# Causal attention in an eight-batch transformer block: the diagonal mask moves from TensorE to GpSimd, and the row maximum is found in two parts

## What is computed

```
def _L1_attn_ref(x, Wq, Wk, Wv, Wo, bo, rel_emb):
    NUM_HEADS, CLIP = 16, 16
    q, k, v = ...                       # x @ W, split into 16 heads of 16 features
    dist = jnp.clip(jnp.abs(r[None, :] - r[:, None]), 0, CLIP)
    scores = jnp.einsum('bhqd,bhkd->bhqk', q, k) * rel_emb[dist]
    causal = jnp.triu(jnp.ones((s, s), dtype=bool), k=1)
    scores = jnp.where(causal, -jnp.inf, scores)
    attn = jax.nn.softmax(scores / np.sqrt(hd), axis=-1)
    ctx = jnp.einsum('bhqk,bhkd->bhqd', attn, v)
    return ctx @ Wo + bo
```

## Time and profile before

| | |
|---|---|
| median of 3 runs | 3185.65 us |
| the profiled execution: its own time | 3191.0 us |
| its span, first to last instruction | 3189.3 us |
| mean granted clock of PE | 0.946 |
| the mask products of the attention phase touched | 512, from 2334.8 to 2857.6 us of the span |

### The profile page before, as it was taken

How to read it: one execution, slowest core, us unless ns; L and a number is a source line. 1 busy time by engine, 2 the same in 40 slices (tenths; PEclk the granted TensorE clock), 3 DMA queues, 4 the chain that set the end, 5 groups by cost and what they waited for, 6 DMA issues and landing times. The chain is left out here.

```text
span 3189.3 us, 54032 instructions
## 1 busy us (share of the span) xinstructions
PE 2881.4 (90%) x19465; PEld 2047.0 (64%) x19465; DVE 1665.2 (52%) x4524; ACT 1528.2 (48%) x2579; POOL 1339.6 (42%) x1331
## 2 busy tenths in 40 slices
PE   4899999767899999668999997999879999988999
PEld 4799999722344333257999996666546666655666
DVE  4411111168888888554111111566676666655666
ACT  1133333247988888611333332333247777772333
POOL 3544444358999999435444443000043444320000
PEclk9899999978999999868999998999989999999999
DMA  8199999800544444861999997100052333301000
GB/s 281 41 299 327 324 321 327 243 14 14 63 60 59 60 60 60 81 209 41 302 326 323 327 325 240 29 0 0 15 139 71 75 94 98 85 2 37 13 13 20
DMA packets 359983, 431.82 MB, mean 135 GB/s; under 512 B 86449, under 2 KB 314694, under 8 KB 356678
## 3 DMA queue, kind: packets, MB, share of 16 engines
q1 hardware_dynamic: 335174, 395.17, 44.5%
q0 software_dynamic: 24576, 33.57, 5.0%
HBM read 355.80 MB, written 72.88 MB: 134 GB/s over the span
## 5 line engine op out<-in xcount | busy, mean ns | idle before, releaser
L1675 ACT ACTIVATE f_h_t<-f_h_ps,f_b_t 128x128 f32<-128x128 f32 x1024 | 319.4, 363 | 601.2 <-PE f_h_ps L1633 596.2
L2069 POOL TENSOR_TENSOR a_dmg_buf<-a_c 128x2048 f32<-128x2048 f32 x128 | 520.1, 4090 | 63.8 <-PE a_dmg_ps L2117 34.0
L1633 PEld LDWEIGHTS f_h_ps<-f_rows_t,f_w 128*128 128x128 f32 x4096 | 482.7, 194 | 9.9 <-issue 3.5
L1633 PE MATMUL f_h_ps<-f_rows_t,f_w 128*128 128x128 f32 x4096 | 483.9, 277 | 2.3 <-DVE f_rows_t L1687 1.2
L1647 PE MATMUL f_y_ps<-f_w,f_h_t 128*128 128x256 f32 x2048 | 483.5, 379 | 0.0
L1593 POOL DMA_INDIRECT acc_rows<-f_y,f_give x128 | 205.0, 1602 | 491.5 <-DMA acc_rows<-f_y,f_give 460.3
L1647 PEld LDWEIGHTS f_y_ps<-f_w,f_h_t 128*128 128x128 f32 x2048 | 369.9, 190 | 39.9
L1687 DVE COPY f_rows_t<-f_t_ps 128x256 f32<-128x256 f32 x128 | 54.3, 425 | 602.3 <-PE f_t_ps L1621 597.6
L2434 DVE SCALAR_TENSOR_TENSOR a_bond_buf<-a_a,a_small_rep,a_q_ps 128x512 f32<-128x512 f32 x512 | 346.6, 740 | 7.4 <-PE a_q_ps L2234 5.1
L428 DVE SCALAR_TENSOR_TENSOR x_resid<-f_y_ps,f_gate,x_resid 128x256 f32 x512 | 218.9, 479 | 163.6 <-PE f_y_ps L311 158.0
L885 ACT ACTIVATE a_prob<-a_prob,a_neg_top 128x384 f32<-128x384 f32 (+3 forms) x512 | 276.6, 570 | 47.1 <-POOL a_neg_top L702 46.9
(11 more groups left out here) (353 smaller groups left out, 4174.6 us busy)
## 6 DMA issues: line engine op xcount, KB each, us to landing
f_w<-in_L_ffn_w_dram SPq DMA_DIRECT2D x256, 1024.0 KB
a_skewed<-skew SPq DMA_DIRECT2D x32, 512.0 KB, 6.8
a_k_s<-parts SPq DMA_DIRECT2D x16, 768.0 KB, 7.9
acc_rows<-x_resid SPq DMA_DIRECT2D x17, 512.0 KB, 5.3
xn_rows<-f_xn SPq DMA_DIRECT2D x16, 512.0 KB, 3.0
x_resid<-acc_rows SPq DMA_DIRECT2D x16, 512.0 KB, 7.4
a_vals<-val_rows SPq DMA_DIRECT2D x64, 128.0 KB, 3.8
skew<-a_bond SPq DMA_DIRECT2D x128, 64.0 KB, 10.2
```

The costliest lines, as they stand in the source:

```text
L1633: last = nc.tensor.matmul(h_ps[n // HB][:, (n % HB) * P:(n % HB + 1) * P], w1_sb[s][:, c, n * P:(n + 1) * P], rows_t[e % 2][:, c, :], star ...
L1675: nc.scalar.activation(h_t[k][:, n, :], h_ps[n // HB][:, (n % HB) * P:(n % HB + 1) * P], ACT.Gelu, bias=b1_t[:, n, e:e + 1]).then_inc(gelu ...
L2069: nc.gpsimd.tensor_tensor(dmg_buf[n % RING][:, :, :], places(c_sb[h], first_place(dg)), c_sb[h][:, PAD:].unsqueeze(1).broadcast_to([P, DG, ...
```

## The change

The mask product L779 goes. DVE multiplies the blocks below the diagonal with the custom instruction (maximum in `top_whole`) and the diagonal block alone with a plain product; POOL masks that block in `prob` with an affine select; DVE then takes its maximum (`find_top`), and POOL's `negate` joins the two maxima. For t = 0 there is only the diagonal block. The distances between the hands grow by two, and the ring by one slot. The two DVE casts that made the bf16 mask and identity go as well.

```diff
-    SCORES_AT, TTR_AT, NEG_AT, EXP_AT = 7, 5, 4, 2
-    PR = 9
+    SCORES_AT, TTR_AT, MASK_AT, TOP_AT, NEG_AT, EXP_AT = 9, 7, 6, 5, 4, 2
+    PR = 10
...
             def negate(u):
-                pool.wait_ge(s_taken, UNIT_USE[u] + 1)
+                group, t, g = unit(u)
+                at = slice(u % PR, u % PR + 1)
+                pool.wait_ge(top_ready, u + 1)
                 if u >= PR:
                     pool.wait_ge(exp_ready, u - PR + 1)
-                nc.gpsimd.tensor_scalar(neg_top[:, u % PR:u % PR + 1], top[:, u % PR:u % PR + 1], -1.0, None,
-                                        ALU.mult).then_inc(top_negated, 1)
+                if t == 0:
+                    nc.gpsimd.tensor_scalar(neg_top[:, at], top[:, at], -1.0, None, ALU.mult).then_inc(top_negated, 1)
+                else:
+                    nc.gpsimd.tensor_scalar(neg_top[:, at], top[:, at], top_whole[:, at], -1.0, ALU.max,
+                                            ALU.mult).then_inc(top_negated, 1)
+
+            def mask(u):
+                group, t, g = unit(u)
+                block = prob[:, u % PR, t * P:(t + 1) * P]
+                pool.wait_ge(s_taken, UNIT_USE[u] + 1)
+                nc.gpsimd.affine_select(out=block, in_=block, compare_op=ALU.is_ge, fill=MASKED, base=0,
+                                        pattern=[[-1, P]], channel_multiplier=1).then_inc(masked, 1)
...
             for s in range(-TTR_AT, ALL):
-                if s + NEG_AT < ALL and s + NEG_AT >= 0:
+                if 0 <= s + MASK_AT < ALL:
+                    mask(s + MASK_AT)
+                if 0 <= s + NEG_AT < ALL:
                     negate(s + NEG_AT)
...
-                                 k_s[half % QK][0:ROWS, h, 0:width], start=True, stop=False)
-                nc.tensor.matmul(bank[:, t * P:width], ident_b[:, :], mask_b[:, :], start=False,
-                                 stop=True).then_inc(s_ready, 1)
+                                 k_s[half % QK][0:ROWS, h, 0:width], start=True, stop=True).then_inc(s_ready, 1)
...
-                nc.vector.tensor_copy(mask_b[:, :], mask_f)
-                nc.vector.tensor_copy(ident_b[:, :], core.ident[:, :])
...
-                nc.vector.tensor_tensor_reduce(
-                    out=prob[:, u % PR, 0:width], in0=s_ps[use % SB][:, 0:width], in1=factor[:, S - width:S],
-                    scale=1.0, scalar=-3.0e38, op0=ALU.mult, op1=ALU.max,
-                    accum_out=top[:, u % PR:u % PR + 1]).then_inc(s_taken, 1)
+                if t:
+                    nc.vector.tensor_tensor_reduce(
+                        out=prob[:, u % PR, 0:t * P], in0=s_ps[use % SB][:, 0:t * P], in1=factor[:, S - width:S - P],
+                        scale=1.0, scalar=-3.0e38, op0=ALU.mult, op1=ALU.max,
+                        accum_out=top_whole[:, u % PR:u % PR + 1])
+                nc.vector.tensor_tensor(prob[:, u % PR, t * P:width], s_ps[use % SB][:, t * P:width], factor[:, S - P:S],
+                                        ALU.mult).then_inc(s_taken, 1)
+
+            def find_top(u):
+                group, t, g = unit(u)
+                dve.wait_ge(masked, u + 1)
+                nc.vector.tensor_reduce(top[:, u % PR:u % PR + 1], prob[:, u % PR, t * P:(t + 1) * P],
+                                        AX.X, ALU.max).then_inc(top_ready, 1)
...
                 if s + TTR_AT < ALL:
                     multiply(s + TTR_AT)
+                if 0 <= s + TOP_AT < ALL:
+                    find_top(s + TOP_AT)
```

More of the change, by code:

```diff
@@ L566, in attn1_phase @@
         factor = sb("factor", [P, S])
-        mask_b = sb("mask_b", [P, P], BF16)
-        ident_b = sb("ident_b", [P, P], BF16)
         stats = sb("stats", [P, TILES, 6])
@@ L586, in attn1_phase @@
         hit = [prob[:, 3 + k, 0:NEAR] for k in range(2)]
-        mask_f = prob[:, 5, 0:P]
+        top_whole = sb("top_whole", [P, PR])
         top = sb("top", [P, PR])
@@ L610, in attn1_phase @@
         q_loaded, k_loaded = sem("q_loaded"), sem("k_loaded")
-        mask_made = sem("mask_made")
         consts = sem("consts")
@@ L622, in attn1_phase @@
         s_taken = sem("s_taken")
+        masked = sem("masked")
+        top_ready = sem("top_ready")
         top_negated = sem("top_negated")
@@ L721, in _ @@
             for s in range(-TTR_AT, ALL):
-                if s + NEG_AT < ALL and s + NEG_AT >= 0:
+                if 0 <= s + MASK_AT < ALL:
+                    mask(s + MASK_AT)
+                if 0 <= s + NEG_AT < ALL:
                     negate(s + NEG_AT)
                 i, m = divmod(s, UNITS)
-                if i < 0:
-                    continue
-                if m < TPB:
+                if i >= 0 and m < TPB:
                     add_bias(i, m)
-                if NORMALISE_AT <= m < NORMALISE_AT + TPB and i + 2 < B:
+                if i >= 0 and NORMALISE_AT <= m < NORMALISE_AT + TPB and i + 2 < B:
                     normalise(i + 2, m - NORMALISE_AT)
```

## The result

The changed kernel takes 3205.73 us (median of 5 runs, 3196.80 to 3208.11), against 3185.65 before: with a ratio of 1.0055 (taken over all the runs, not from the two medians, which are 20 us apart) and a 95% interval of 1.0042 to 1.0067. That is 17.5 us slower (13 to 21). The time lies in the range I gave, but the forecast "no change" was not the case that came; it is where the third case, VectorE as the bound, was put at 3205.

A forecast was written before the change was run, and what follows sets the result against it. PE was taken to set the pace in places, ACT in others, and DVE at the start. The terms -18 + 7 + 8 + 3 sum to 0, so 3186 us on the median, range 3166 to 3212.

The forecast's parts named there:

- the forecast "no change": Whole kernel: PE's gain and DVE's cost cancel, 3186 us within 6.4 either way; chance 0.34.
- the third case: Rival: DVE becomes the bound with 60 us of work and 7 of waiting per batch, 3205 us; chance 0.22.
- PE's term: Attention loop: 512 mask products leave PE, at most 30 us; 60% taken as paid out, 18 us less.
- What a unit costs on DVE: Split product and second maximum on DVE: 0.06 plus 0.21, together 0.27 us per unit, 17 us per batch.
- The start: First 27 units, where DVE has no room: the added 0.27 us each comes fully on the path, 7 us more.
- DVE in the loop: Steady loop: four banks absorb most of DVE's lag, 1 us a batch leaks, 8 us in all.
- behind the normalising pieces: POOL's select comes late where a normalising piece stands behind select and sign: 0.5 us in six batches, 3 us.
- the sentence that the exponential has its sign as many steps ahead as now: Lookahead on the score path: it grows by two steps while the sign's lead in steps stays; no cost was added.
- The fourth one: Rival: POOL's select is late in each step, 0.6 us each, POOL the bound at 3195 to 3225 us; chance 0.12.

The follow-up runs named there:

- the one with one maximum: Changed kernel with DVE's custom instruction and maximum over the whole width again, no second maximum, POOL still masking; ratio 0.9986 to the kernel before.
- the kernel with the short distances: Changed kernel with a single maximum over the whole unmasked width, and the distances and nine slots of the kernel before; ratio 1.0002 to the kernel before.
- without mask product: Kernel before with its mask product removed and nothing in its place, so the output differs; ratio 0.9971 to the kernel before.
- with the pieces spread: Changed kernel with a single maximum and long distances, POOL's four normalising pieces in every second step instead of four steps running; ratio 0.9992 to the kernel before.

## Why the prediction was right or wrong

The range held, and the forecast case did not come. I had said that gain and loss cancel; slower was given 0.34, as much as no change, and came. The range was 46 us wide, so that it held says little about the sum: two terms of the sum were too small and one gain too large.

**PE's term.** The step is "I take 60%: 18 us less". Alone it is 1.6 us a batch, 13 us over eight, and 9 us by the ratio. The reading of the earlier trace rows was right in kind, that PE's product is not paid out in full; the share was too high, and in the changed kernel the same product is worth only 0.7 us a batch.

**What a unit costs on DVE.** 0.21 us for each piece was taken; 0.20 and 0.19 were measured. The split of a four-block unit costs 0.48 + 0.20 - 0.61 = 0.07 us, where the sum took 0.09. Together it was 0.24 us a unit and not 0.27. By the figures of the Trainium skill ("VectorE: DVE Perf Modes", section on the TRN2 errata), an estimate, the reduction is 194 ns and a split 125 ns. The first agrees with the measured 0.19 us; for the second the trace has 0.07 us, and the trace decides.

**The start.** 7 us were forecast; the last statistics come 7.9 us later.

**DVE in the loop.** The step is "most is absorbed and a little leaks: 8 us in all". Its work alone, the difference between the changed kernel and the one with one maximum, is 1.6 us a batch, about 12 us in the loop. I had counted room in batches, 23 us of it. In the changed kernel DVE is busy for 57.6 us of the 67.3, so it has 9.7 us free in each batch and the batch is longer all the same. What counts is, as I read it, how late DVE is within a group, against four banks and against the lead of the sign.

**GpSimd.** "3 us" behind the normalising pieces: there it is nothing. Instead the select costs 1.6 us a batch once PE's product is gone, about 12 us in all, and what grows with it in the waits is the exponential's wait for the sign (45.8 us in the kernel with the short distances, 19.1 without mask product). This is the largest miss of the sum. The step that failed is the sentence that the exponential has its sign as many steps ahead as now. In steps that is so; in time the sign now ends 0.70 us ahead of its exponential on average where it was 1.40. Behind DVE's product there come a select of 296 ns and a sign with two inputs of 293 ns, where there was a sign of 209 ns, and DVE is later besides.

**The rivals.** The fourth one named the select, but as work that fills POOL, with 0.6 us for each. It takes 296 ns, and POOL is busy for 36.65 of 50 us. The third one, DVE as the bound, was put at 67 us a batch and 3205 us, which is nearly what was measured, and its start of 7 us was right. Its batch was 60 us of work and 7 us of waiting; measured are 57.6 of work and 9.7 without, of which only about 1.1 are waits for scores (8.3 in 500 us). It has neither PE's gain nor the select, 13 and 12 us, which happen to cancel. So its closeness is in part luck.

The sum by batch, from the marks: 65.7 as before; without the product 64.1; with the select 65.6, with the new distances as well 65.7; with the split and the second maximum 67.3. Times eight, and with the start, that is -13 + 12.5 + 12.5 + 8 = 20 us. The profiled executions are 15.4 us apart at the last copy, since the first batch gives something back and the last is shorter. Over the profiled execution: +7.9 us to the first mark, -2.3 in the first batch, +8.2 in the next five, +1.7 from there to the last copy of the values (2864.9 before, 2880.3 now), 15.4 of the span's 15.8.

Besides how DVE's 1.6 us come about, two things stay open. The group that holds the normalising pieces is 16.8 us with the long distances and a select, 15.4 in the kernel without product; spreading the pieces left it at 16.8, so it is not that they follow one another, and what it is I did not isolate. And the gain of the first batch is only seen, not explained.

Of all versions, the one with one maximum over the unmasked scores is the fastest that computes the reference, by 0.14% (0.02 to 0.25), less than what I called no change. With the short distances the ratio was 1.0002 and with the pieces spread 0.9992, so whether it is faster at all is not settled.

## What to carry to other kernels

Room that is counted over a whole period says little for an engine that works in order with few buffers: 0.2 us a unit on an engine busy 66% of the time, ahead of the release of its buffer, cost as much as the whole change. Where an instruction leaves the engine that sets the pace, ask which chain gets it: here it went into the chain from score to exponential, where half of the sign's lead in time was used up though its steps stayed the same. Look which instruction the late one really stands behind: the idle time ahead of each group showed that it was the select of a later unit and not the reduction. A softmax maximum need only be an upper bound, so it can be taken before the mask, and then the second maximum isn't needed. That holds as long as the masked scores don't exceed the kept ones by so much that the exponentials become zero.

## What was not expected of the hardware

GpSimd's sign with two inputs of one column took 293 ns against 217 for the one-input form in the same run. Sets of runs of one kernel, three of them on three different chips, differed by up to 12 us in their medians (3185.65 and 3198.0 for the kernel before), while the distance of two marks within one trace of that kernel repeated to 0.1 us.
